# One of four inverse-length multiplies moves from VectorE to GpSimd, in a newly searched order of tasks

## What is computed

```python
def _layer(x, wqkv, qs, ksc, wo, lg, lb, w1, b1, w2, b2):
    h = shift_token(x)
    q, k, v = jnp.split(h @ wqkv, 3, axis=-1)       # 8 heads of 64
    q = l2norm(q) * qs
    k = l2norm(k) * ksc
    q, k = rotary_xpos(q, k)
    o = local_attention(q, k, v)                    # windows of 64, this one and the one before
    x = x + o @ wo
    h = shift_token(x)
    ...                                             # layer norm, then a gated GELU feed-forward
    return x + h @ w2 + b2
```

## Time and profile before

| | us |
|---|---|
| median of three runs | 2657.15 |
| lowest and highest of them | 2637.15 and 2661.07 |
| the profiled execution | 2653.83 |
| its span, first to last instruction | 2652.0 |
| TensorE busy in the span | 2361.2 |
| VectorE busy | 1973.2 |
| ScalarE busy | 1663.7 |
| GpSimd busy | 971.3 |

### The profile page before, as it was taken

How to read it: one execution, slowest core, us unless ns; L and a number is a source line. 1 busy time by engine, 2 the same in 40 slices (tenths; PEclk the granted TensorE clock), 3 DMA queues, 4 the chain that set the end, 5 groups by cost and what they waited for, 6 DMA issues and landing times. The chain is left out here.

```text
span 2652.0 us, 59877 instructions
## 1 busy us (share of the span) xinstructions
PE 2361.2 (89%) x20669; PEld 1587.4 (60%) x20796; DVE 1973.2 (74%) x4686; ACT 1663.7 (63%) x3472; POOL 971.3 (37%) x1094
## 2 busy tenths in 40 slices
PE   4998989898989899469999999999999999999981
PEld 3665656565656566346666666666666666666641
DVE  3676767676767677476878787878878878888846
ACT  1554545454445445356878777877868777888845
POOL 2111101010111111174646464645555646565502
PEclk9999999999999999778999999999999999999995
DMA  2000000000000000011011001010101010110104
GB/s 78 1 5 6 5 6 5 6 5 6 5 6 5 6 5 5 29 33 36 20 27 24 22 16 30 22 24 24 42 16 30 15 29 16 29 28 15 29 1 127
DMA packets 32177, 55.75 MB, mean 21 GB/s; under 512 B 3472, under 2 KB 23104, under 8 KB 29888
## 3 DMA queue, kind: packets, MB, share of 16 engines
q1 hardware_dynamic: 31936, 52.38, 7.9%
HBM read 13.70 MB, written 8.39 MB: 8 GB/s over the span
## 5 line engine op out<-in xcount | busy, mean ns | idle before, releaser
L370 ACT ACTIVATE a_probs<-a_st 128x512 f32<-128x512 f32 x640 | 381.3, 599 | 479.9 <-PE a_st L578 477.7
L466 DVE TENSOR_REDUCE a_qpack<-a_s 128x1 f32<-128x512 f32 (+3 forms) x704 | 439.4, 639 | 196.5 <-PE a_s L566 188.9
L987 POOL TENSOR_TENSOR b_part_b<-b_raw,b_tabs 128x256 f32<-128x256 f32 x512 | 432.1, 874 | 332.2 <-ACT b_raw L1046 297.7
L996 POOL TENSOR_TENSOR b_qk<-b_qk,b_part_b 128x1024 f32<-128x1024 f32 x128 | 332.4, 2597 | 281.6 <-DVE b_qk L1153 274.3
L565 PE MATMUL a_s<-a_kT,a_qT 128*128 128x512 f32 (+3 forms) x1024 | 367.2, 410 | 66.5 <-DVE a_qpack L466 27.2
L577 PE MATMUL a_st<-a_qmT,a_kT 128*128 128x512 f32 (+3 forms) x1024 | 364.2, 401 | 4.4 <-ACT a_qmT L357 0.7
L324 POOL TENSOR_TENSOR a_turned<-a_qkv,a_cos 128x640 f32<-128x640 f32 x16 | 24.8, 1548 | 812.0 <-DVE a_z L486 761.9
L565 PEld LDWEIGHTS a_s<-a_kT,a_qT 128*128 128x128 f32 x1024 | 204.0, 202 | 180.3 <-DVE a_qpack L466 114.7
L1153 DVE TENSOR_TENSOR b_qk<-b_raw,b_tabs 128x512 f32<-128x512 f32 x256 | 282.0, 1141 | 0.1
L566 PE MATMUL a_s<-a_mask_ts,ident_bf 128*128 128x128 bf16 x1024 | 232.4, 235 | 0.0
L578 PE MATMUL a_st<-a_mask_st,ident_bf 128*128 128x128 bf16 x1024 | 227.9, 233 | 0.0
(11 more groups left out here) (193 smaller groups left out, 5233.6 us busy)
## 6 DMA issues: line engine op xcount, KB each, us to landing
b_v_even<-b_v SPq DMA_DIRECT2D x32, 528.0 KB, 4.4
b_v_even<-b_v SPq DMA_DIRECT2D x32, 396.0 KB, 5.8
x_scratch<-a_x SPq DMA_DIRECT2D x16, 256.0 KB, 2.3
out<-c_y SPq DMA_DIRECT2D x4, 1024.0 KB, 5.4
b_w_raw<-in_L_ffn_wqkv SPq DMA_DIRECT2D x2, 768.0 KB, 4.3
b_tabs<-tab SPq DMA_DIRECT2D x2, 512.0 KB, 4.1
b_w_raw<-in_L_ffn_w SPq DMA_DIRECT2D x4, 170.5 KB
b_wo<-in_L_ffn_wo SPq DMA_DIRECT2D x2, 256.0 KB
```

Of the source, the lines that this page charges most:

```text
L370: act.activation(probs[:, j % 2, k, :], st_bank[:, UNIT_BANK[k], :], ACT.Exp, scale=SCALE1).then_inc(probs_made, 1)
L466: dve.tensor_reduce(qpack[:, slot, i, j, gs[0]:gs[-1] + 1, NEG_MAX], s_bank[:, (j * NCH + c) % 2, 0:w * len(gs)].rearrange("p (g s) -> p g ...
L987: last = pool.tensor_tensor(part_b[:, x, :].rearrange("p (h d) -> p h d", d=DH)[:, :, lo:lo + DH // 2], raw[:, i % 2, x, :].rearrange("p ( ...
L996: pool.tensor_tensor(qk[:, i], qk[:, i], part_b[:], ALU.add).then_inc(c_made, 1)
```

## The change

The tile i = 3 is multiplied by GpSimd and no longer by VectorE; tiles 0 to 2 stay. GpSimd waits for the last `rope_add` of the sequence and for `newton`, and raises a new semaphore, `last_scaled`, for which `turn_q` 3 waits. `scaled` now counts three a sequence. `FIRST_ROPE`, the task ahead of which the tables are loaded, is now looked up as the first rope task of tile 0. And `ORDER` is another list: the same 153 tasks in another sequence, with other banks and, for some, in another part.

```diff
-FIRST_ROPE = next(name for _, name, *_ in ORDER if name in ("rope_cos", "rope_sin"))
+FIRST_ROPE = min((part, at, name) for at, (part, name, arg, *_) in enumerate(ORDER)
+                 if name in ("rope_cos", "rope_sin") and arg == 0)[2]
...
+        def scaled_by(eng, i):
+            a = qk[:, i].rearrange("p x (h d) -> p (x h) d", d=DH)
+            lengths = rs[:, i * 16:(i + 1) * 16].rearrange("p (h a) -> p h a", a=1).to_broadcast([P, 16, DH])
+            return eng.tensor_tensor(a, a, lengths, ALU.mult)
...
+            def scale(l, b, i, slot):
+                if i < TT - 1:
+                    return
+                pool.wait_ge(c_made, (seq(l, b) + 1) * TT)
+                pool.wait_ge(dve_step, PLAN.own_steps("newton", 0, l, b) + OWN_STEPS["newton"])
+                scaled_by(pool, i).then_inc(last_scaled, 1)
...
             def scale(l, b, i, slot):
+                if i == TT - 1:
+                    return
                 dve.wait_ge(c_made, seq(l, b) * TT + i + 1)
...
+                scaled_by(dve, i).then_inc(scaled, 1)
...
             def turn_q(l, b, i, slot):
-                pe.wait_ge(scaled, seq(l, b) * TT + i + 1)
+                if i < TT - 1:
+                    pe.wait_ge(scaled, seq(l, b) * (TT - 1) + i + 1)
+                else:
+                    pe.wait_ge(last_scaled, seq(l, b) + 1)
```

The head of the new list, and its end, with the places that matter:

```diff
+    (1, "copy_k", 1), (1, "rope_sin", 3), (0, "h", 0), (1, "rope_add", 3), (1, "turn_q", 2, "o"), (0, "low", 0),
+    (1, "copy_q", 2), (2, "values", 4, "x"), (2, "p_turn", 6, "w1"), (2, "divide", 4), (2, "o_turn", 1, "o"),
+    (1, "scale", 3), (2, "copy_o", 0), (0, "project_q", 0, "w0"), (2, "copy_p", 6), (2, "copy_o", 1),
+    (0, "project_k", 0, "w1"), (0, "square", 0), (0, "raw_q", 0), (2, "values", 5, "o"), (2, "values", 6, "x"),
+    (2, "divide", 5), (1, "turn_q", 3, "o"), (2, "divide", 6), (0, "raw_k", 0), (0, "project_q", 1, "w0"),
...
+    (0, "rope_sin", 0), (0, "square_sums", 1), (2, "out", 0, "x"), (1, "row_max", 1), (2, "out", 1),
+    (0, "rope_add", 0), (1, "exp", 1), (2, "out", 2), (0, "square", 2), (2, "copy_o", 3), (0, "rope_sin", 1),
+    (0, "raw_q", 2), (2, "out", 3), (0, "rope_cos", 1), (1, "exp", 2), (1, "p_turn", 0, "w0"), (0, "square_sums", 2),
+    (0, "project_v", 0, "o"), (0, "raw_k", 2), (1, "p_turn", 1, "w1"), (1, "copy_p", 0), (0, "copy_v", 0),
+    (2, "residual", 0), (0, "rope_add", 1), (1, "copy_p", 1), (0, "rope_cos", 2), (1, "exp", 3),
+    (0, "project_q", 3, "w0"), (2, "stat_turn", 0, "x"), (0, "project_k", 3, "w1"), (0, "square", 3),
+    (1, "scores", 2, "sa"), (2, "variance", 0), (1, "row_max", 2), (1, "p_turn", 2, "o"), (0, "raw_q", 3),
+    (0, "square_sums", 3), (2, "rstd_seed", 0), (2, "rstd", 0), (0, "project_v", 1, "w0"), (1, "values", 0, "x"),
+    (0, "raw_k", 3), (0, "project_v", 2, "w1"), (0, "rope_sin", 2), (1, "copy_p", 2), (0, "copy_v", 1),
+    (1, "values", 1, "o"), (1, "divide", 0), (1, "exp", 4), (0, "limit", 0), (0, "copy_v", 2),
+    (2, "rstd_turn", 0, "w0"), (0, "seed", 0), (1, "divide", 1), (1, "scores", 3, "sb"), (2, "normalise", 0),
...
+    (2, "gate", 0, "x"), (2, "gate", 1, "w0"), (1, "divide", 2), (2, "gelu", 0), (2, "gate", 2, "o"), (2, "gelu", 1),
+    (0, "scale", 0), (2, "gelu", 2), (2, "hidden", 0, "w1"), (1, "row_max", 3), (1, "p_turn", 4, "x"),
+    (1, "copy_p", 4), (2, "product", 0), (0, "scale", 1), (0, "turn_q", 0, "w0"), (0, "rope_add", 2),
+    (2, "hidden", 1, "o"), (2, "product", 1), (1, "values", 3, "x"), (2, "down", 0, "w1"), (0, "copy_q", 0),
+    (1, "divide", 3), (0, "scale", 2), (0, "turn_q", 1, "w0"), (2, "hidden", 2, "o"), (0, "project_v", 3, "x"),
+    (2, "down", 1), (1, "exp", 6), (0, "copy_q", 1), (1, "exp", 7), (2, "product", 2), (0, "turn_k", 0, "w0"),
+    (0, "rope_cos", 3), (1, "p_turn", 5, "o"), (2, "down", 2), (0, "copy_v", 3), (0, "turn_k", 1, "x"),
+    (2, "result", 0), (0, "copy_k", 0), (1, "copy_p", 5), (1, "o_turn", 0, "w0"),
```

More of the change, by code:

```diff
@@ L667 @@
 ORDER = [
[L668 to L687, removed]
@@ L688 @@
-    (0, "raw_k", 3), (0, "project_v", 3, "w1"), (1, "copy_p", 2), (2, "normalise", 0), (1, "values", 1, "o"),
-    (2, "gate", 0, "w0"), (0, "copy_v", 2), (0, "limit", 0), (0, "copy_v", 3), (1, "row_max", 3), (0, "seed", 0),
-    (0, "rope_sin", 3), (1, "divide", 1), (0, "newton", 0), (2, "gelu", 0), (1, "p_turn", 3, "w1"), (0, "scale", 0),
-    (2, "gate", 1, "x"), (1, "o_turn", 0, "o"), (2, "hidden", 0, "w0"), (2, "product", 0), (2, "gelu", 1),
-    (1, "copy_o", 0), (2, "gate", 2, "x"), (0, "turn_q", 0, "o"), (1, "copy_p", 3), (2, "hidden", 1, "w1"),
@@ L693 @@
-    (2, "gelu", 2), (0, "scale", 1), (0, "copy_q", 0), (2, "product", 1), (2, "hidden", 2, "w0"), (2, "down", 0, "o"),
-    (1, "exp", 5), (2, "product", 2), (0, "turn_k", 0, "w1"), (0, "copy_k", 0), (1, "p_turn", 4, "x"), (1, "exp", 6),
-    (2, "down", 1), (0, "rope_cos", 3), (2, "down", 2), (0, "scale", 2), (0, "rope_add", 3), (1, "p_turn", 5, "w1"),
-    (1, "copy_p", 4), (0, "turn_q", 1, "w0"), (1, "values", 2, "x"), (2, "result", 0), (1, "divide", 2),
-    (0, "copy_q", 1),
+    (1, "copy_k", 1), (1, "rope_sin", 3), (0, "h", 0), (1, "rope_add", 3), (1, "turn_q", 2, "o"), (0, "low", 0),
@@ new lines @@
+    (1, "copy_q", 2), (2, "values", 4, "x"), (2, "p_turn", 6, "w1"), (2, "divide", 4), (2, "o_turn", 1, "o"),
+    (1, "scale", 3), (2, "copy_o", 0), (0, "project_q", 0, "w0"), (2, "copy_p", 6), (2, "copy_o", 1),
+    (0, "project_k", 0, "w1"), (0, "square", 0), (0, "raw_q", 0), (2, "values", 5, "o"), (2, "values", 6, "x"),
+    (2, "divide", 5), (1, "turn_q", 3, "o"), (2, "divide", 6), (0, "raw_k", 0), (0, "project_q", 1, "w0"),
+    (1, "turn_k", 2, "w1"), (1, "copy_q", 3), (1, "turn_k", 3, "x"), (1, "copy_k", 2), (2, "p_turn", 7, "o"),
@@ new lines @@
+    (0, "square_sums", 0), (0, "project_k", 1, "w1"), (1, "copy_k", 3), (0, "rope_cos", 0), (2, "copy_p", 7),
+    (1, "scores", 0, "sa"), (2, "values", 7, "x"), (1, "row_max", 0), (2, "divide", 7), (2, "o_turn", 2, "o"),
+    (0, "square", 1), (0, "raw_q", 1), (0, "raw_k", 1), (1, "scores", 1, "sb"), (2, "copy_o", 2),
+    (2, "o_turn", 3, "o"), (1, "shift_v", 0), (1, "exp", 0), (0, "project_q", 2, "w0"), (0, "project_k", 2, "w1"),
+    (0, "rope_sin", 0), (0, "square_sums", 1), (2, "out", 0, "x"), (1, "row_max", 1), (2, "out", 1),
@@ new lines @@
+    (1, "exp", 5), (1, "p_turn", 3, "o"), (1, "values", 2, "w1"), (1, "copy_p", 3), (0, "newton", 0),
+    (2, "gate", 0, "x"), (2, "gate", 1, "w0"), (1, "divide", 2), (2, "gelu", 0), (2, "gate", 2, "o"), (2, "gelu", 1),
+    (0, "scale", 0), (2, "gelu", 2), (2, "hidden", 0, "w1"), (1, "row_max", 3), (1, "p_turn", 4, "x"),
+    (1, "copy_p", 4), (2, "product", 0), (0, "scale", 1), (0, "turn_q", 0, "w0"), (0, "rope_add", 2),
+    (2, "hidden", 1, "o"), (2, "product", 1), (1, "values", 3, "x"), (2, "down", 0, "w1"), (0, "copy_q", 0),
@@ L1008, in h @@
                 pool.tensor_copy(h_high[:], ds_u(b, slice(0, P), slice(0, T))).then_inc(high_made, 1)
-            walk(pool, dict(rope_sin=rope_sin, rope_add=rope_add, h=h))
+            walk(pool, dict(rope_sin=rope_sin, rope_add=rope_add, h=h, scale=scale))
         @block.scalar
```

7 lines of the change are left out of this document (2 added, 5 removed).

## The result

The changed kernel takes 2761.66 us (median; 2748.47 to 2763.54 over four runs), the kernel before 2659.11 beside it: 1.039 times as long, interval 1.033 to 1.046, so it is slower. Every ratio in this text is to the kernel before, run beside the kernel in question; the same kernel's median moved between 2652 and 2659 us from one group of runs to the next, so small differences are read from the ratios. The profiled execution has a span of 2760.2 us against 2652.0, 108 us more.

What follows compares the result with a forecast made beforehand. TensorE, busy 98% of an undisturbed step, was taken as the bound; 31 steps x (-0.5 for waits removed + 0.4 for the variance chain) = -3, and +1 for a table reload, gave 2652 us, range 2626 to 2692.

Runs made afterwards that it cites:

- e7: Changed kernel with rope_add 2 held until after rstd, raw_k 3 and divide 1 moved earlier, and waits shifting both layers' loop code: 2644.28 us, ratio 0.998.

## What to carry to other kernels

When an order changes, price each VectorE instruction on a path to the bound engine twice, free and beside the GpSimd instruction that the new order puts next to it: a tensor_scalar of four numbers costs the rest of a 2.4 us addition. Follow each other engine's queue past the instruction that waits, for what stands behind it needs no part in the dependency to be late. And read the branch rows of a hardware loop before comparing two orders: four per cent of this result was in two parts, and some two fifths of it were long branches, most of which went in e7 when the loops' code was shifted.
